# First attention layer: exponentials stored as 16-bit integers

## What is computed

```python
def _fq_unsigned(x, axis):
    s = jnp.max(x, axis=axis, keepdims=True) / 255.0
    s = jnp.maximum(s, 1e-08)
    q = jnp.clip(jnp.round(x / s), 0.0, 255.0) * s
    return x + jax.lax.stop_gradient(q - x)
...
attn = jnp.einsum('bhqd,bhkd->bhqk', q, k)
attn = jax.nn.softmax(attn.astype(jnp.float32), axis=-1)
attn = _fq_unsigned(attn, axis=-1)
out = jnp.einsum('bhqk,bhkd->bhqd', attn, v)
out = jnp.transpose(out, (0, 2, 1, 3)).reshape(B, N, C)
return out @ Wp + bp
```

## Time and profile before

| | us |
|---|---|
| median of 3 runs | 2335.09 (2330.97 to 2339.15) |
| the profiled execution: its own time | 2333.09 |
| its span, first to last instruction | 2331.3 |
| PE busy over the span | 1749.9 |
| DVE busy over the span | 1245.6 |
| ACT busy over the span | 849.2 |
| POOL busy over the span | 714.1 |
| the head loop, first to last instruction | about 92 to 357 |

### The profile page before, as it was taken

One profiled execution on the slowest core, in us unless ns is written; L12 is line 12 of the kernel. 1 busy time (PEld: TensorE's weight loads), 2 busy tenths in 40 slices (PEclk: granted clock), 3 DMA queues, 4 the chain that ended last, 5 costly groups with the idle time before them and its releaser, 6 DMA issues. The chain is left out here.

```text
span 2331.3 us, 28461 instructions
## 1 busy us (share of the span) xinstructions
PE 1749.9 (75%) x8489; PEld 1094.2 (47%) x8492; DVE 1245.6 (53%) x2738; ACT 849.2 (36%) x2046; POOL 714.1 (31%) x1414
## 2 busy tenths in 40 slices
PE   5677764998783599991698989888499878726663
PEld 4322223555452355551355556556255566525442
DVE  4889982223553422227577878778322345652222
ACT  1866661111221111112366666667211144402221
POOL 0123320000100000005777788776000020007884
PEclk8655555999686699995799999999699978857887
DMA  1277771110003111102000000000111000066866
GB/s 61 47 130 137 131 129 46 34 40 20 1 1 145 39 52 58 58 30 64 10 1 0 0 0 0 0 0 0 31 34 34 20 27 0 0 242 155 205 137 144
DMA packets 180391, 132.09 MB, mean 57 GB/s; under 512 B 141986, under 2 KB 163490, under 8 KB 177235
## 3 DMA queue, kind: packets, MB, share of 16 engines
q1 hardware_dynamic: 160370, 104.40, 17.1%
q0 software_dynamic: 12976, 20.46, 4.8%
q10 hardware_dynamic: 6960, 6.19, 0.8%
HBM read 81.62 MB, written 15.83 MB: 42 GB/s over the span
## 5 line engine op out<-in xcount | busy, mean ns | idle before, releaser
L1327 PE MATMUL l2x_pr<-l_w,l2x_xs 128*128 128x512 f32 x512 | 250.2, 614 | 81.2 <-POOL l2x_xs L1285 81.2
L1734 ACT ACTIVATE l0m_pf<-l0m_s,l0m_bias,l0x_sq 128x1024 f32<-128x1024 f32 x128 | 154.1, 1204 | 86.2 <-POOL l0m_bias L1675 86.1
L1754 DVE TENSOR_REDUCE l0m_mx<-l0m_s 128x1 f32<-128x1024 f32 x128 | 155.6, 1217 | 34.1 <-PE l0m_s L1687 33.9
L259 PE MATMUL l1e_gu<-x_normT,l1e_w 128*128 128x512 f32 x384 | 170.8, 598 | 3.2 <-DMA l1e_w<-in_l_ffn 3.0
L1327 PEld LDWEIGHTS l2x_pr<-l_w,l2x_xs 128*128 128x128 f32 x512 | 93.2, 195 | 156.3 <-issue 151.1
L1675 POOL TENSOR_SCALAR l0m_bias<-l0m_mx,l0x_nsq 128x1 f32<-128x1 f32 x128 | 78.7, 615 | 266.6 <-DVE l0m_mx L1754 265.2
L1687 PE MATMUL l0m_s<-l0x_kT,l0x_qT 48*128 48x512 bf16 x256 | 131.6, 618 | 6.9 <-PEq L1499 4.1
L1451 DVE TENSOR_SCALAR l2x_raw<-l2x_raw,l2x_mv,l2x_rs 128x128 f32<-128x128 f32 x384 | 128.0, 396 | 15.2 <-POOL l2x_rs L1306 15.2
L300 DVE TENSOR_TENSOR l1e_h<-l1e_sil,l1e_gu 128x512 f32<-128x512 f32 x48 | 33.0, 688 | 182.5 <-ACT l1e_sil L285 169.8
L1441 DVE BATCH_NORM_STATS2 l2x_bn<-l2x_raw 128x6 f32<-128x128 f32 x384 | 83.3, 278 | 86.5 <-ACT l2x_raw L1390 86.4
L259 PE MATMUL l0e_gu<-x_normT,l0e_w 128*128 128x512 f32 x272 | 121.3, 600 | 9.0 <-DMA l0e_w<-in_l_ffn 9.0
(11 more groups left out here) (465 smaller groups left out, 3988.7 us busy)
## 6 DMA issues: line engine op xcount, KB each, us to landing
l3m_w<-in_l_moe SPq DMA_DIRECT2D x16, 1280.0 KB, 7.4
l1e_w<-in_l_ffn SPq DMA_DIRECT2D x24, 384.0 KB, 2.9
l_w<-in_l_w SPq DMA_DIRECT2D x4, 2048.0 KB, 14.8
l0e_w<-in_l_ffn SPq DMA_DIRECT2D x17, 384.0 KB, 3.0
l2e_w<-in_l_ffn SPq DMA_DIRECT2D x16, 384.0 KB, 2.9
l1e_route<-l_route SPq DMA_DIRECT2D x8, 512.0 KB
l2q_wps<-in_l_wp SPq DMA_DIRECT2D x16, 256.0 KB, 2.6
l_w<-l_acc SPq DMA_DIRECT2D x16, 256.0 KB, 4.9
```

The source lines that it names most:

```text
L259: last = nc.tensor.matmul(gu[half][:, m, :], w[:, slot, (2 * k + m) * P:(2 * k + m + 1) * P], pg.xnT[:, k, half * HALF:(half + 1) * HALF], ...
L1327: last = nc.tensor.matmul(flat(pr[t % 2][:]), xs[:, side, src, k, :], w[:, k, (side * 8 + t) * W:(side * 8 + t + 1) * W], start=(k == 0), ...
L1734: nc.scalar.activation(pf[:, n % 4, :], s_ps[n % 3][:], ACT.Exp, scale=sq[:, b, h:h + 1], bias=bias[:, n % 4:n % 4 + 1], accum_out=sm[:, b ...
L1754: nc.vector.tensor_reduce(mx[:, n % 4:n % 4 + 1], s_ps[n % 3][:], AX, ALU.max).then_inc(s["maxed"], 1)
```

## The change

The tile `pf` becomes int16 (four buffers of 1024), so ScalarE converts the exponential to a 16-bit integer as it writes. The rounding by addition and subtraction becomes a copy from `pf` to `pi`, int16 to bf16, on VectorE. The waits, the semaphores, the number of buffers and the order stay as they are, and so does the row sum, which ScalarE's accumulator still gives in float32.

```diff
--- before.py
+++ after.py
@@ -1637,7 +1637,7 @@
                 return st.enter_context(nc.psum_tensor(f"l0m_{m}", shape, dt))
             mx = sb("mx", [P, 4])
             bias = sb("bias", [P, 4])
-            pf = sb("pf", [P, 4, T])
+            pf = sb("pf", [P, 4, T], I16)
             pi = sb("pi", [P, 4, T], BF16)
             pT = sb("pT", [P, 4, B, P], BF16)
             sm = sb("sm", [P, 2, H])
@@ -1757,7 +1757,7 @@
                     dve.wait_ge(s["exped"], n + 1)
                     if n >= 4:
                         dve.wait_ge(moved[n % 4], 16 * (n // 4))
-                    nc.vector.tensor_scalar(pi[:, n % 4, :], pf[:, n % 4, :], ROUND, ROUND, ALU.add, ALU.subtract).then_inc(s["rounded"], 1)
+                    nc.vector.tensor_copy(pi[:, n % 4, :], pf[:, n % 4, :]).then_inc(s["rounded"], 1)
 
                 def scale(b):
                     dve.wait_ge(s["exped"], H * b + H)
```

## The result

Nine runs of each: 2321.8 us median (2316.4 to 2328.1) against 2337.9 (2331.0 to 2340.2), a ratio of 0.9935 with a 95% interval of 0.9922 to 0.9948. That is 16 us by the medians, 12 to 18 by the interval. The forecast was 21.6 us (2313.5 against 2335.1), the range 2303 to 2326.

What follows compares the result with a forecast made beforehand. VectorE was taken to bound the head loop, at 1.733 us a plain step. Plain steps 19.0 + boundaries 6.3 - late transposes 3.5 = 21.8 us gained, giving a median of 2313.5 us; range 2303 to 2326.

Steps and rivals of the forecast that it cites:

- rival 1: Head loop: the 16 DMA engines bind at 1.56 us a transpose; gain 19 to 8 us, 2316 to 2327; chance 0.12.
- plain steps above 1.55 us: Head loop: a sign that the forecast is wrong; plain steps exceeding 1.55 us would mean the DMA engines bind.
- DMA share of a quiet stretch: Head loop: the DMA engines' busy share in a quiet stretch, 0.90 before, was to be about 1.
- VectorE sets the pitch before, DMA after: Head loop's plain steps: VectorE sets 1.73 us before; afterwards the loop through the transposes, at 1.52, is longer than VectorE's 1.479.
- four-step loop: Head loop: rounding, transpose, value matmuls, next score, maximum, rounding again; 6.33 us over four heads, to become 6.08.
- The copy at 0.427: VectorE in the head loop: the int16-to-bf16 copy takes 0.427 us against the rounding's 0.681, saving 0.254 us a head.
- Rivals 2 and 3: VectorE's copy: either slow at 1.219 us, 2398 us in all, chance 0.09; or unchanged at 0.681, 2335 us, chance 0.07.
- The bias near 0.39: GpSimd in the head loop: the bias, 0.64 us before, was to take near 0.39 us behind the shorter copy.
- Boundaries 12.17: Boundary of each group of 16 heads: 13.07 us becomes 12.17, 0.90 by 7 boundaries, 6.3 us gained.
- The plain step of 1.52: Head loop: 90 plain steps go from 1.733 to 1.52 us, held by the transposes; 19.0 us gained.
- Late transposes: Head loop: with no slack left, late landings cost about 5 us in place of 1.5, giving 3.5 us back.
- Rival 4: TensorE in the head loop: its granted clock rises from 1.2 to 2.4 GHz; gain 38 us, 2297; chance 0.04.

Runs made afterwards that it cites:

- e1: Changed kernel with value matmuls one more step behind the scores (LAG 6, not 5): 2304.5 us median, 0.9862 of before; first to last maximum 221.5 us.
- e11: Kernel before the change (float32 exponentials and rounding) with LAG 6 in place of 5: first to last maximum 249.9 us, against 251.2.
- e5: Changed kernel run again unaltered: 2324.6 us median, 0.9942 of before; first to last maximum 237.75 us.
- e2: Changed kernel with each transpose half the size, half of each head's weights left out: first to last maximum 225.7 us, against 236.7.
- e6: Changed kernel with LAG 6 in place of 5, run a second time: 2307.9 us median, 0.9879 of before; first to last maximum 221.8 us.
- e8: Changed kernel with LAG 6, plus a 64-element VectorE memset behind each copy: first to last maximum 222.1 us, against 221.5 without the memset.
- e10: Changed kernel with LAG 6, plus a 160-element VectorE memset behind each copy: first to last maximum 232.0 us, 10.3 more than without.
- e4: Changed kernel with sixteen already fulfilled waits a head in GpSimd's queue behind the bias: first to last maximum 238.7 us, against 236.7.

## Why the prediction was right, and where it fell short

The direction and the mechanism hold; the size is off by 8.3 us (2321.8 against 2313.5). The measured time is inside the range, but in the part that lies in rival 1's 2316 to 2327 as well, and the range reached up to 2326 for that rival's sake. So the time alone doesn't tell the forecast from the rival: e1 does. One of the forecast's own signs of being wrong came true: plain steps above 1.55 us, which it put down to the engines. Undisturbed ones take 1.575, and e1 shows that the reading of that sign was wrong, not the loop that binds. The DMA share of a quiet stretch (206 to 224 us) is 0.92, where about 1 was forecast.

- *VectorE sets the pitch before, DMA after.* Right. e11 shows the first (the lag gives nothing while the rounding is slow), e1 the second. The forecast's "1.52, not 1.48" was right in kind, and e1 shows it: with the four-step loop opened the plain step is 1.47.
- *The copy at 0.427.* 0.419. Rivals 2 and 3 are out. ScalarE's output to int16 costs nothing: 1.204 against 1.204.
- *The bias near 0.39:* 0.37.
- *Boundaries 12.17:* 12.15 in a typical one, 5.6 us gained over all seven, 6.3 forecast; one of them (13.46 us) was lengthened by a late transpose, by more than the one that was so before (13.52 in place of 13.07). In all they take 86.4 us for a forecast of 85.2.
- *The plain step of 1.52.* This term was mis-sized. The forecast's sum of 6.08 us kept the transpose at the 3.1 us it took when transposes came 1.73 apart. Eleven plain steps on from that boundary, with no fetch between:

```profile
247.78 1.22 DVE L1754 TENSOR_REDUCE l0m_mx<-l0m_s 128x1 f32<-128x1024 f32 x1
```

From 230.46, the last row of the boundary above, that is 17.32 us, 1.575 a step (1.570 in the same stretch of e5). The median landing is 3.3 us, and 6.08 + 0.2 over four is 1.57. The loop runs in bursts of steps at VectorE's pace, then a wait, so transposes are issued 1.47 apart and crowd each other. By the times of the trace, those without a fetch beside them land in a median of 3.36 us when they are issued within 1.55 us of the one before, and in 3.19 when 1.7 us or more behind it; in e1 it is 3.38 and 3.09, in e2, with half the size, 2.42 in both. Worth 90 by 0.053 = 4.8 us.
- *Late transposes.* 5 us were forecast in plain steps. 148.1 less 141.7 (90 by 1.575) is 6.4 (in e5, 8.7). The forecast counted landings alone. A part of the lateness lies ahead of them, in SyncE: an issue keeps it 1.23 us, but up to 2.58 in the changed kernel when a fetch runs beside it, and the next copies then wait for their issue, which else starts 0.45 us after the copy does:

```profile
298.88 2.58 SPq L1666 DMA_TRANSPOSE l0m_pT<-l0m_pi  x1
...
299.90 0.42 DVE L1760 CAST l0m_pi<-l0m_pf 128x1024 bf16<-128x1024 int16 x1
...
301.55 1.26 SPq L1666 DMA_TRANSPOSE l0m_pT<-l0m_pi  x1
```

Of the 106 issues over 1.4 us in the 14 traces, 103 have a fetch beside them. In none of them do two issues of whole transposes follow each other within less than 1.32 us, so at a pitch of 1.47 the lost time is made up slowly: the three copies from 299.90 on get their issues 1.65, 1.53 and 1.45 us after their start.
- *Rival 1, the DMA engines bind.* Half right. Transposes do crowd, which is what the 0.2 us are. But they don't bind at 1.56 us: with LAG 6 they go through every 1.47 us for whole stretches, at a busy share above one (this row is of e6).

```profile
197.00:209.00 12.00, 9.84 (x77) 3.09 (x73) 11.46 (x17) 10.00 (x17) 2.96 (x8) 0.50 1.08 170
```

The share of busy time over 16 engines reaches 1.08, so it counts packets in flight side by side, and dividing it by the pitch, as rival 1 did, says nothing of capacity.
- *Rival 4, the clock.* 0.50 in the changed kernel and with LAG 6 too, with TensorE busy 9.84 of the 12 us in that last row. That activity releases the throttle, as the Trainium skill has it (TensorE: Matmul & The Clock Gate, Part 1), isn't seen in any run of this loop.
- *The contention of which the Trainium skill speaks* (GPSIMD Engine Reference, Key points) hits GpSimd alone here: the bias, started inside the copy, ends 0.13 us after it, as before, and the copy's slowest of 128 is 0.427 us.

Sum: forecast 21.8, measured 14.5 in the loop, 236.7 us in place of 229.4: 4.8 for the landing time, 1.4 for late transposes in plain steps and 1.2 at boundaries make up the 7.3.

## What to carry to other kernels

When the engine that sets the pitch is made faster, work out the next loop with the latencies that it will have at the new pitch, not the old: a DMA's landing time grows when its neighbours come closer, and a delay that slack used to absorb is then paid in full. Here one more step of lag, which alone was worth 1.3 us, returned 15 to 16 us behind the faster copy. A probe that is to load an engine has to be seen in the start times of its neighbours before its result is read.

## What the runs showed of the hardware that was not expected

- A VectorE memset of 64 elements, 0.112 us by the profile, adds about 0.01 us to the step (e8); one of 160 elements, 0.192 us, adds 0.11 (e10).
- Transposes of 128 x 1024 two-byte elements go through every 1.47 us at a median landing of 3.4 us, while at a pitch of 1.73 they land in 3.1; half-size ones land in 2.4.
- Fetching instructions takes time on the DMA engines: packets of 16 KB take 0.9 to 1.9 us, and 161 of the 282 transposes with one in flight in their first 3 us land over 0.7 us late (before the change up to 4.8 us in place of 3.1), against 7 of 1236 without any fetch.
- SyncE's issue of a transpose takes 1.23 us, and up to 2.75 (e4) with a fetch beside it; two issues are never less than 1.32 us apart (1.28 with half the size, e2).
